# Letting the sums of a graph aggregation lag three steps behind the expansion instead of two

## The reference, cut to what matters

```python
def _sage_conv(x, src, dst, Wl, Wr, b):
    agg = jax.ops.segment_sum(x[src], dst, num_segments=N)
    cnt = jax.ops.segment_sum(jnp.ones((src.shape[0],), x.dtype), dst, num_segments=N)
    mean = agg / jnp.maximum(cnt, 1.0)[:, None]
    return mean @ Wl.T + b + x @ Wr.T
h = jnp.maximum(_layernorm(x, axis=-1), 0.0)
h = jax.nn.relu(_sage_conv(h, src, dst, W1l, W1r, b1))
x = x + _sage_conv(h, src, dst, W2l, W2r, b2)
```

## Time and profile before

| what | value |
|---|---|
| time, median of 3 runs | 4431.24 us |
| the runs | 4424.57 to 4433.46 us |
| span of the profiled execution | 6409.5 us |
| PE, busy share of the span | 4496.5 us, 70% |
| DVE | 3802.5 us, 59% |
| POOL | 2916.3 us, 45% |
| ACT | 1895.0 us, 30% |

### The profile page before, as it was taken

The page is one execution under the profiler, slowest core; times in us unless marked ns, Lnnn a source line. Parts: engine busy times, 40 slices in busy tenths (PEclk is TensorE's granted clock), DMA queues, the critical chain, the costliest instruction groups (busy, mean ns, idle before and its releaser), DMA issues. The chain is left out here.

```text
span 6409.5 us, 172985 instructions
## 1 busy us (share of the span) xinstructions
PE 4496.5 (70%) x64703; PEld 4078.8 (64%) x64703; DVE 3802.5 (59%) x6756; ACT 1895.0 (30%) x4426; POOL 2916.3 (45%) x2761
## 2 busy tenths in 40 slices
PE   3888888877888886465666666666666666666667
PEld 3777777776777776455555555565555555555557
DVE  7888888886666666454445444444444444454456
ACT  3555554544444443221111111111111111111112
POOL 2666666634444445244444443444444344444430
PEclk8999999999999998667767766776766677677777
DMA  4333333324333332333333333333333333333322
GB/s 87 77 78 77 76 75 75 76 70 128 87 88 90 89 88 58 87 101 92 95 88 99 90 95 90 92 97 92 95 89 93 88 95 95 91 98 92 95 82 55
DMA packets 481486, 562.00 MB, mean 88 GB/s; under 512 B 180610, under 2 KB 437873, under 8 KB 480870
## 3 DMA queue, kind: packets, MB, share of 16 engines
q1 hardware_dynamic: 395782, 451.91, 26.4%
q0 software_dynamic: 84032, 103.47, 7.0%
q10 hardware_dynamic: 1266, 0.31, 0.0%
HBM read 478.48 MB, written 76.90 MB: 87 GB/s over the span
## 5 line engine op out<-in xcount | busy, mean ns | idle before, releaser
L1352 POOL DMA_INDIRECT sorted_edges<-edge_rows,edge_index x1566 | 1527.0, 975 | 2150.2 <-ACT edge_rows L1451 1726.8
L969 POOL DMA_INDIRECT conv_got<-parts_table,conv_index x1060 | 1256.9, 1186 | 834.5 <-issue 240.2
L1413 PE MATMUL edge_sums<-edge_parts,edge_hot 128*128 128x64 bf16 (+1 forms) x15582 | 870.4, 219 | 863.8 <-issue 665.7
L1413 PEld LDWEIGHTS edge_sums<-edge_parts,edge_hot 128*128 128x128 bf16 x15582 | 734.7, 115 | 970.2 <-issue 789.6
L1081 ACT CAST conv_rows<-conv_rows_ps 128x384 bf16<-128x384 f32 x2226 | 998.7, 458 | 1124.4 <-PE conv_rows_ps L995 951.6
L995 PE MATMUL conv_rows_ps<-parts,conv_hot_t 128*128 128x192 bf16 x8268 | 1083.4, 252 | 349.0 <-ACT conv_rows L1081 163.1
L1549 DVE TENSOR_TENSOR edge_a_ps<-edge_a_ps,edge_edges 128x448 f32<-128x448 f32 x371 | 233.8, 630 | 1842.6 <-PE edge_a_ps L1398 939.0
L1012 PE MATMUL conv_sums<-conv_rows,conv_hot_d 128*128 128x193 bf16 (+1 forms) x8268 | 1084.0, 252 | 3.7 <-DMA conv_got<-parts_table,conv_index 2.5
L1398 PE MATMUL edge_a_ps<-parts,edge_hot_t 128*128 128x64 bf16 x15582 | 801.0, 220 | 311.4 <-issue 295.7
L995 PEld LDWEIGHTS conv_rows_ps<-parts,conv_hot_t 128*128 128x128 bf16 x8268 | 686.1, 99 | 470.4 <-ACT conv_rows L1081 209.8
L1398 PEld LDWEIGHTS edge_a_ps<-parts,edge_hot_t 128*128 128x128 bf16 x15582 | 714.5, 117 | 376.0 <-issue 360.4
(11 more groups left out here) (189 smaller groups left out, 4383.8 us busy)
## 6 DMA issues: line engine op xcount, KB each, us to landing
edge_slot_row<-slot_rows SPq DMA_DIRECT2D x371, 224.0 KB
edge_edges<-sorted_edges SPq DMA_DIRECT2D x371, 224.0 KB
conv_slot_row<-slot_rows SPq DMA_DIRECT2D x424, 192.0 KB
conv_slot_row<-slot_rows SPq DMA_DIRECT2D x318, 160.0 KB
edge_dst_row<-dst_rows SPq DMA_DIRECT2D x261, 192.0 KB
edge_attr<-in_edge_attr SPq DMA_DIRECT2D x260, 192.0 KB
sorted_edges<-edge_rows,edge_index POOLq DMA_INDIRECT x1566
conv_got<-parts_table,conv_index POOLq DMA_INDIRECT x1060
```

The source lines that it names most:

```text
L969: pool.indirect_dma_start(got[g][:, f, 0:PARTS * D], None, k.parts_table, bass.IndirectOffsetOnAxis(ap=index[h][:, g, at:at + 1], axis=0)) ...
L1352: pool.indirect_dma_start(k.sorted, bass.IndirectOffsetOnAxis(ap=index[h][0:used, at:at + 1], axis=0), rows[j][0:used, t, :], None).then_i ...
L1413: mm = pe.matmul(to[:, 0:n], hot[at][:, u, v * P:(v + 1) * P], parts[at][:, u, i, 0:n], start=(i == 0), stop=(i == PARTS - 1), skip_group_ ...
```

## The change

In both aggregations the sum of a step comes three steps behind its expansion (`behind` = 3) instead of two. Expansion i waits for the copy of step i-3, and both aggregations have three banks. `rows` has five buffers, given out by `place_of`. The first three sums of a block's end are made in the next block's steps 0, 1 and 2.

The bank for the third `rows_ps` in the first aggregation comes from `row_ps`, which becomes the upper half of `count_ps`. `count` therefore waits until the row of two blocks before was taken (`row_made`). The table `tile_rows`, which POOL made at the start, goes; its matrices (row t all ones, the others zero) are read as weights from one column of the identity, repeated 128 times with a step of zero.

```diff
-        self.row_ps = o.psum("row_ps", [P, 1024], BF16)
+        self.row_ps = self.count_ps[:, 256:512].bitcast(BF16)
@@ count
+        if n >= 2:
+            wait_alone(pe, self.row_made, c - 1)
@@ prefix
-            if n == 0:
-                pe.wait_ge(self.tables_made, 1)
-            mm = pe.matmul(to[:, t - j * PT, :], self.tile_rows[:, t, :], self.earlier[:], ...)
+            mm = pe.matmul(to[:, t - j * PT, :], self.k.ident_b[0:BT, t:t + 1].to_broadcast([BT, P]), self.earlier[:], ...)
@@ conv
-        bs, cut, banks, bufs, most = NG * ns, 8, 2 if sorting else 3, 3, (GU - min(fetched)) * P
+        bs, cut, banks, behind, most = NG * ns, 8, 3, 3, (GU - min(fetched)) * P
+        place_of = [i % (behind + 1) if i < 4 * (behind + 1) else i - 4 * (behind + 1) for i in range(bs)]
-        rows = several(bufs, o.tmp, "rows", [P, 2, PARTS * D + 2], BF16)
+        rows = several(max(place_of) + 1, o.tmp, "rows", [P, 2, PARTS * D + 2], BF16)
@@ gpsimd
-            if sorting:
-                pool.tensor_copy(s.tile_rows[:], wide(k.ident_b[0:BT, 0:BT], 2, [BT, BT, P])).then_inc(s.tables_made, 1)
@@ expand
-                if n >= 1 or i >= 2:
-                    pe.wait_ge(copied, bs * b + i - 1)
+                if n >= 1 or i >= behind:
+                    pe.wait_ge(copied, bs * b + i + 1 - behind)
@@ first
-                        if i < 2 and n >= 1:
-                            reduce(b - 1, 1 - h, n if n == MANY else n - 1, bs - 2 + i)
-                        if i >= 2:
-                            reduce(b, h, n, i - 2)
+                        if i < behind and n >= 1:
+                            reduce(b - 1, 1 - h, n if n == MANY else n - 1, bs - behind + i)
+                        if i >= behind:
+                            reduce(b, h, n, i - behind)
```

More of the change, by code:

```diff
@@ L644, in __init__ @@
         self.number = pair(o.tmp, "number", [P, 3, BT, QUAD], BF16)
-        self.earlier, self.tile_rows = o.tmp("earlier", [BT, SRC_WINDOWS], BF16), o.tmp("tile_rows", [BT, BT, P], BF16)
+        self.earlier = o.tmp("earlier", [BT, SRC_WINDOWS], BF16)
         self.ranks = o.tmp("ranks", [P, BT, SRC_WINDOWS], BF16)
@@ L657, in __init__ @@
             "rank_taken", "rank_kept", "rank_spread", "slot_hot_made", "scattered", "slots_taken", "row_turned", "row_made")
-        self.tables_made, self.row_stored, self.missed_summed, self.step = o.sems("tables_made", "row_stored", "missed_summed", "sort_step")
+        self.row_stored, self.missed_summed, self.step = o.sems("row_stored", "missed_summed", "sort_step")
     def spread_numbers(self, act, c, h, n):
@@ L723, in prefix @@
         for t in tiles:
-            mm = pe.matmul(to[:, t - j * PT, :], self.tile_rows[:, t, :], self.earlier[:], start=False, stop=(t == tiles[-1]), skip_group_check=True)
+            mm = pe.matmul(to[:, t - j * PT, :], self.k.ident_b[0:BT, t:t + 1].to_broadcast([BT, P]), self.earlier[:], start=False, stop=(t == tiles[-1]), skip_group_check=True)
         mm.then_inc(self.ranked, 1)
@@ L856, in conv @@
         ns = len(steps[0])
-        bs, cut, banks, bufs, most = NG * ns, 8, 2 if sorting else 3, 3, (GU - min(fetched)) * P
-        assert all(len(s) == ns for s in steps) and 2 * bs % banks == 0 and bs % bufs == 0
+        bs, cut, banks, behind, most = NG * ns, 8, 3, 3, (GU - min(fetched)) * P
+        place_of = [i % (behind + 1) if i < 4 * (behind + 1) else i - 4 * (behind + 1) for i in range(bs)]
+        assert all(len(s) == ns for s in steps) and 2 * bs % banks == 0 and banks >= behind
+        assert all(place_of[i] != place_of[i - n] for i in range(bs) for n in range(1, behind + 1))
         s = Sorting(k, o) if sorting else None
@@ L942, in _ @@
             pool.memset(k.acc[:], 0.0).then_inc(begun, 1)
-            if sorting:
-                pool.tensor_copy(s.tile_rows[:], wide(k.ident_b[0:BT, 0:BT], 2, [BT, BT, P])).then_inc(s.tables_made, 1)
-            else:
+            if not sorting:
                 pool.memset(zero[:], 0.0).then_inc(zero_made, 1)
@@ L1005, in reduce @@
                     pe.wait_ge(summed, b - 1)
-                here = [(u, rows[i % bufs][:, u - u0, 0:wide_cols]) for u in range(u0, u1)]
+                here = [(u, rows[place_of[i]][:, u - u0, 0:wide_cols]) for u in range(u0, u1)]
                 if i % ns == ns - 1 and fetched[g]:
@@ L1066, in _ @@
             in_turn(pe, first, second)
-            for i in (bs - 2, bs - 1):
+            for i in range(bs - behind, bs):
                 pe.wait_ge(copied, bs * (NB - 1) + i + 1)
@@ L1080, in copy_rows @@
                 act.wait_ge(expanded, bs * b + i + 1)
-                act.copy(rows[i % bufs][:, 0:n, 0:PARTS * D], rows_ps[(bs * h + i) % banks][:, 0:n * PARTS * D].rearrange("p (u d) -> p u d", u=n)).then_inc(copied, 1)
+                act.copy(rows[place_of[i]][:, 0:n, 0:PARTS * D], rows_ps[(bs * h + i) % banks][:, 0:n * PARTS * D].rearrange("p (u d) -> p u d", u=n)).then_inc(copied, 1)
             def take_dst(b, h, n):
```

## The result

The kernel after takes 4471.28 us (median of 4 runs, 4468.27 to 4494.48) against 4432.35 before; the ratio is 1.0093, 95% interval 1.0069 to 1.0117. Run again on another chip it took 4460.92 us (10 runs) against 4432.57, ratio 1.0062 (1.0038 to 1.0087). It is slower, as forecast, by 28 to 39 us where +35 was predicted. Executions of every kernel here lie on two levels some 25 us apart, with a few between, and one execution of experiment 11 that took 4867 us is left out; a median can fall on either level, so kernels are compared by stages in traces or on one level. A ratio is always to the kernel before, run on the same chip: experiments 1 to 4 ran on one chip, 5 to 8 on a second, 9 to 12 on a third.

A forecast was written before the change was run, and what follows sets the result against it. Bounds: POOL's issues in the edge loop, DVE and PE holding each other in the first aggregation, PE alone in the second. 0 + 34 + 4 + 0 - 2.5 = +35 us, 4431 + 35 = 4466; range 4375 to 4495.

The forecast's parts named there:

- The budget from the edge loop's issues: Timed 4431 us less 504 for other stages and 1989 for POOL's issues leaves both aggregations 1940 to 2000.
- The second aggregation, 0: Longer lag in the second aggregation: PE alone is the bound, its matmuls stay the same, 0 us in timed runs.
- The lag in the first aggregation, +34: First aggregation: DVE's wait for step 14's sums and PE's block start lengthen, 0.67 us a block, +34 us.
- The two signs: Next profile, first aggregation: DVE's wait before `hot_d` grows from 66.5 us by 20 or more; `hot_t` ends expansion 0's stall.
- The six matmuls: First aggregation: PE does six more matmuls before the sums of step 14 that DVE awaits, 0.50 us a block.
- the first `scatter`: Start of a first-aggregation block: PE reaches it behind 16 matmuls instead of 18, waiting 0.17 us more for `slots`.
- The wait before `count`, +4: First aggregation: always met, costs only register and semaphore work on PE's sequencer, +4 us, bounds 0 and 8.
- The weights, 0: 1530 PE weight loads with a step of zero keep their 91 ns: 0 us; slow end 204 us.
- The table's start, -2.5: Kernel start: without POOL's 3.37 us copy, DVE's first `members` is quicker; -2.5 us once, bounds 0 and -3.4.
- A: Rival: late PE signals are in timed runs too and the longer lag softens them, -25 to -70 us, 4385; chance 0.22.
- B: Rival: DVE's wait has slack in timed runs and the terms cancel, 4431 within 9 us; chance 0.18.
- C: Rival: zero-step weight loads each take 25 to 100 ns longer, 38 to 153 us on top, 4530; chance 0.08.

The follow-up runs named there:

- experiment 11: Kernel after (lag of three) with the three `scatter` pieces behind steps 2, 3 and 5 instead of 1, 2 and 4; 4461.35 us, ratio 1.0057.
- experiment 1: The control: kernel before, unchanged, profiled a second time; 4429.38 us.
- experiment 2: Kernel after with the lag of two and three `rows` buffers back in the first aggregation alone; 4402.15 us, ratio 0.993.
- experiment 3: Kernel after (lag of three) with `sum_chosen` moved ahead of `hot_d` of group 6 on DVE; 4401.45 us, ratio 0.9906.
- experiment 4: Kernel after (lag of three) with a fourth buffer for `hot_d`; 4390.61 us, ratio 0.9891.
- experiment 5: Kernel after, unchanged, run again on a second chip; 4460.92 us.
- experiment 6: Kernel before with only the table's part changed: identity columns as weights; table, copy, semaphore and wait gone; 4401.57 us, ratio 0.9931.
- experiment 7: Kernel after with the lag of two in the first aggregation and the table, its copy and semaphore put back; 4434.03 us, ratio 0.9993.
- experiment 8: Kernel after with the lag of two in the first aggregation and `sum_chosen` ahead of `hot_d` of group 6; 4376.93 us, ratio 0.9865.
- experiment 9: Experiment 6's kernel with one unused semaphore allocated where the table's was; 4399.02 us, ratio 0.9928.
- experiment 10: Experiment 6's kernel with the table and POOL's copy into it put back, read by nobody, no semaphore; 4430.54 us, ratio 1.0014.
- experiment 12: Kernel after with the lag of two in the first aggregation, a fourth `hot_d` buffer and `sum_chosen` ahead of `hot_d` of group 6; 4392.15 us, ratio 0.993.

## Why the prediction was right, and where it was not

**Reading the trace.** The budget from the edge loop's issues said that timed executions have no room for the stalls on copies. The control confirmed it: no such wait is left with the lag of two, and its blocks are the 21.2 us that the prediction worked out. The budget's terms were off and cancelled in part, which was luck: the edge loop takes 2032 us where 1989 was put, and the other stages 432 where 504 was, which leaves 1141 + 823 = 1964 us for the aggregations, inside the 1940 to 2000. This step carried the sign; priced from the earlier trace rows, the change would have looked like a gain of 100 us or more. What the prediction cites from the Trainium skill's "NOTIFIC — the notification-queue block", section 7.1, stays open: the second recording had no late signals, so recording alone does not make them, and no run here shows the block.

**The second aggregation, 0.** Measured +0.9 us in the traces. Its blocks are 15.2 us with either lag, not the 16.0 of the budget, whose source, PE's 877 us, was itself stretched (800 in the control).

**The lag in the first aggregation, +34.** Right in place and way, DVE's wait for the sums of step 14 and the chain of 3.34 us behind it; experiments 3 and 4 remove the loss from either end of that chain. The two signs that it named came: DVE's waits for the sums grew, from 55.2 us in the control to 100.4, and the stall before expansion 0 is ended by `hot_t`. The size was too small: 57 us, 1.1 us a block for 0.67. The six matmuls (0.50) and the first `scatter` (0.17 predicted, 0.16 measured) were right. What I left out is that the sum of step 20 is also awaited: it frees `hot_d` of group 1, and behind that stand the third piece of `slots` and PE's third `scatter` (0.31); and PE now comes to the third piece of `prefix` before ACT has taken the second (about 0.2).

**The wait before `count`, +4.** Not seen: the idle time before `count` is 0.16 us as before, and experiment 2's first aggregation is within 2 us of the control's. **The weights, 0.** Right, 92 ns for 91; the trace agrees with the column steps that the prediction cites from the Trainium skill. **The table's start, -2.5.** The first `members` fell from 3.52 to 0.97 us, and blocks begin 1.2 to 1.6 us earlier, 2.4 in experiment 6.

**Missed altogether:** the edge loop, -29 us by the traces of experiments 1 and 5 and -17 in the first trace. No row of the kernel before could have said so. That the total of +35 came so near is luck: this gain and the 23 us missing from the lag nearly cancel. A, B and C did not come about.

## What to carry to other kernels

Before a stall is priced, set each stage of the trace against a floor from durations that hold in it (here POOL's issues, 0.97 us even in the stretched trace) and the sum against the timed runs; take a second trace if they disagree. A longer software lag moves every release of a buffer back by a step: it is free only where all that wait for those releases, and what stands behind them on their engine, have that step in hand. If an engine idles in a fixed order of work, try filling the idle time with the independent instruction that stands next in line: here one moved reduction took 1.5 us off a block with the lag of three and 0.5 with the lag of two. One more buffer for what the engine waits on did as much or more, 1.8 us with the lag of three.

## What the hardware showed that I had not expected

An edit far ahead of a stage changed the price of its instructions: POOL's indirect issues take 0.973 to 0.976 us on average in nine of the ten traces without the copy into the table and 0.990 to 0.993 in the three quiet traces with it (experiments 1, 7 and 10), some 0.305 us apart in all. Experiments 9 and 10 tie this to the copy or the table's place, not to the semaphore. The medians go the same way, 0.958 to 0.959 against 0.969 us, and the stretched trace of the kernel before, with the copy, has this median too, though its mean is 0.975. The first trace of the kernel after lies between (mean 0.982, median 0.962) and is not explained.

The two levels of time differ after the edge loop: from POOL's last issue to the end of the span it is 117 to 119 us in seven of the quiet traces (the first of the kernel after and experiments 1, 2, 6, 8, 9 and 12), 143 to 145 in five (3, 4, 5, 7 and 10) and 133 in experiment 11. In a trace of the kernel after at 4480.6 us PE's clock is granted at 1.2 GHz (0.50) through the output stage, and in one of experiment 2 at 2.4 for most of it (0.95); columns as in the earlier trace rows:

```profile
4425.00:4450.00 25.00, 25.00 (x123) 25.00 (x122) 9.35 (x18) 5.48 (x6) 0.00 (x0) 0.50 0.20 48
4450.00:4481.00 31.00, 26.32 (x126) 26.13 (x126) 9.98 (x18) 4.57 (x5) 0.00 (x0) 0.50 0.24 58
```

```profile
4370.00:4401.00 31.00, 24.99 (x224) 24.42 (x222) 17.68 (x33) 9.14 (x10) 0.00 (x0) 0.95 0.39 96
```

Ahead of the slow output stage PE was busy for 15 of 25 us at 0.70, ahead of the other for 18 of 30 at 0.77. Why it falls one way or the other was not looked into.
